# Attention output turned and added tile by tile; the second expert's slots placed later

## The reference

```python
# x, ctx: (8, 256, 512); 32 heads of 8 rows
kv  = einsum("bhil,bhjl->bijhl", ctx, ctx)             # all pairs of a head's rows
y   = irfft(rfft(kv, 1024) * rfft(taps, 1024))[:512] + kv * D
out = einsum("bijhl,bhil->bjhl", y, layernorm(x))      # weighed with the query, summed
x   = x + out
t   = layernorm(x)                                     # 2048 tokens of 512
w, i = top_4(softmax(t @ gate_w.T)); w = w / w.sum()   # 16 experts
buf  = the first 256 tokens that chose each expert     # "slots"
y    = scatter_add(w * (silu(t[buf] @ w_gate) * (t[buf] @ w_up)) @ w_down)
x    = x + y + (silu(t @ sw_gate) * (t @ sw_up)) @ sw_down
```

## Time and profile before

| What | Value |
|---|---|
| median of 3 runs | 621.06 us |
| the profiled execution | 620.51 us |
| its span of instructions | 618.4 us, so 2.1 us lie around it |
| mean granted clock of PE | 0.989 |
| PE busy | 586.6 us (95%), 4387 matmuls |
| DVE busy | 487.8 us (79%) |
| POOL busy | 396.7 us (64%) |
| ACT busy | 291.6 us (47%) |
| group 0's heads summed (`oT` of head 3 done) | 43.6 us |
| PE starts the last group's `mixed_out` | 344.3 us |
| PE starts `gate_up(7, 0)` | 354.3 us |
| PE starts `expert_gu(0, 0, 0)` | 384.5 us |
| one expert, from there on | about 14.05 us |

### The profile page before, as it was taken

The page is one execution under the profiler, slowest core; times in us unless marked ns, Lnnn a source line. Parts: engine busy times, 40 slices in busy tenths (PEclk is TensorE's granted clock), DMA queues, the critical chain, the costliest instruction groups (busy, mean ns, idle before and its releaser), DMA issues.

```text
span 618.4 us, 13645 instructions
## 1 busy us (share of the span) xinstructions
PE 586.6 (95%) x4387; PEld 549.2 (89%) x4387; DVE 487.8 (79%) x1277; ACT 291.6 (47%) x521; POOL 396.7 (64%) x502
## 2 busy tenths in 40 slices
PE   3969999999999999999999999999999999999993
PEld 3759988999999989989999797999999999999992
DVE  6988787679779779598698878988888788887640
ACT  2525334434434435345261333666665566566741
POOL 6997988878888888789771363178834433333342
PEclk9989999999999999999999999999999999999997
DMA  6575215136325336152340146778887888888643
GB/s 189 182 249 170 72 69 166 49 85 179 82 80 156 75 93 170 42 140 55 85 111 2 51 160 209 231 246 233 222 239 211 216 237 237 240 226 241 147 53 48
DMA packets 60489, 92.01 MB, mean 149 GB/s; under 512 B 4260, under 2 KB 36004, under 8 KB 60440
## 3 DMA queue, kind: packets, MB, share of 16 engines
q1 hardware_dynamic: 53168, 74.53, 39.4%
q0 software_dynamic: 7168, 16.78, 13.3%
q10 hardware_dynamic: 104, 0.08, 0.1%
HBM read 74.29 MB, written 17.08 MB: 148 GB/s over the span
## 4 chain that ended last, share of the span: by engine, by line
PE 76%; DVE 9%; POOL 6%; issue 4%; ACT 2%; DVEq 1%; DMA 1%; POOLq 0%; SPq 0%; ACTq 0%
PE gu L678 16%; PE gu L827 15%; PE yb L558 11%; PE mb L844 10%; PE gu L716 7%; PE yb L827 6%; PE mb L530 4%; POOL kv L1230 3%; PE yb L530 2%; PE yb L608 2%; DVE oT L1507 2%; DVE prod L1489 2%; DVE prod L1491 1%; POOL kvl L1247 1%; PE yb L798 1%
## 5 line engine op out<-in xcount | busy, mean ns | idle before, releaser
L678 PE MATMUL gu<-xT,sw 128*128 128x256 f32 (+2 forms) x1104 | 136.4, 281 | 0.3 <-issue 0.3
L678 PEld LDWEIGHTS gu<-xT,sw 128*128 128x128 f32 (+2 forms) x1104 | 131.8, 180 | 1.0 <-issue 0.7
L1230 POOL TENSOR_TENSOR kv<-kT 128x256 f32 (+3 forms) x232 | 106.8, 500 | 0.0
L1247 POOL TENSOR_TENSOR kvl<-kv,kvh 128x1440 fp32r<-128x1440 f32 (+1 forms) x28 | 87.7, 3132 | 25.8 <-ACT kvh L954 25.6
L1489 DVE TENSOR_TENSOR prod<-yb,qT 128x64 f32<-128x64 f32 (+10 forms) x272 | 74.8, 286 | 16.4 <-PE yb L608 11.4
L954 ACT ACTIVATE kvh<-kv 128x1440 fp32r<-128x1440 f32 (+1 forms) x28 | 37.5, 1339 | 78.9 <-POOL kv L1237 36.9
L1507 DVE TENSOR_REDUCE oT<-prod 128x256 f32<-128x2048 f32 x32 | 73.0, 2280 | 0.1
L558 PE MATMUL yb<-kvh,tlast 128*128 128x288 f32 x280 | 66.0, 297 | 0.0
L1491 DVE TENSOR_TENSOR prod<-yb,qT 128x96 f32<-128x96 f32 (+10 forms) x238 | 64.2, 270 | 0.0
L844 PE MATMUL mb<-ed,midh 128*128 128x512 f32 x180 | 57.4, 400 | 0.0
L1776 DVE TENSOR_TENSOR ew<-raw_w,ew 128x704 fp32r<-128x704 f32 x64 | 55.1, 882 | 0.3 <-ACT ew L1102 0.3
(11 more groups left out here) (219 smaller groups left out, 1327.4 us busy)
## 6 DMA issues: line engine op xcount, KB each, us to landing
raw_w<-in_L_ffn_w_gate_dram SPq DMA_DIRECT2D x16, 704.0 KB, 7.9
raw_w<-in_L_ffn_w_up_dram SPq DMA_DIRECT2D x16, 704.0 KB, 8.8
raw_d<-in_L_ffn_w_down_dram SPq DMA_DIRECT2D x16, 512.0 KB, 4.3
tlast<-toeplitz_taps SPq DMA_DIRECT2D x20, 384.0 KB, 3.5
tstep<-tap_steps SPq DMA_DIRECT2D x20, 256.0 KB, 4.1
c_t<-in_ctx_dram SPq DMA_DIRECT2D x16, 256.0 KB, 4.8
x_t<-in_x_dram SPq DMA_DIRECT2D x16, 256.0 KB, 4.9
toep<-toeplitz_taps SPq DMA_DIRECT2D x8, 512.0 KB, 3.9
```

Of the source, the lines that this page charges most:

```text
L678: last = pe.matmul(bank[0:m, u * GT:(u + 1) * GT], sw[:, c, a, col:col + m], xT[:, c, b, :], start=(c == 0 and (a, b) == PASSES[0]), stop= ...
L1230: last = pool.tensor_tensor(to[:, :, POFF[d]:POFF[d] + w], src[:, :, 0:w], src[:, :, d * B:HD * B], ALU.mult)
L1247: pool.tensor_tensor(kvl[:, s, 0:nb, :], kv[:, s, 0:nb, :], kvh[:, s, 0:nb, :].bitcast(fp32), ALU.subtract)\
```

## The change

`mixed_out` waits for half of a group's heads before each tile instead of for all of them before both. In the last group tile 0 is transposed ahead of the convolution of the last head (head 31), and DVE adds x to it and takes its first statistics ahead of that head's `multiply`; tile 1 is transposed behind the first 5 of the 17 matmuls of `down(6, [0])`. In group 0 DVE makes the same two steps one behind the other, tile by tile. The statistics of a group are combined once tile 1's are there.

Further on `slots(1)` moves on PE behind the whole of `down(7, [0])` and the first 8 matmuls of `down(7, [1])`. On DVE `one_hot(1)` moves behind the last low part of the shared expert (`low_mid(7, 5)`), `decode(1, 1)` moves behind `chunk_sum(7, [0])`, and `middle(7, 4)` changes places with `low_mid(7, 3)`. Since `mid` has two buffers, `middle` of the last group now also waits for the low part that read its buffer.

```diff
-            def mixed_out(g, nq):
-                pe.wait_ge(d_sum, GH * (g + 1))
-                for t in range(TT):
+            def mixed_out(g, nq, tiles=range(TT)):
+                for t in tiles:
                     wait(pe, q_ev, TT * nq + t + 1)
+                    pe.wait_ge(d_sum, GH * g + (t + 1) * GH // TT)
                     last = transposes(mb[:, t, :], ...)
                     last.then_inc(o_tr, 1)
...
@@ PE, steps(g)
                     gate_up(g - 1, 3)
+                if not prep:
+                    mixed_out(g, g, [0])
                 convolve(GH * g + 3, 3)
@@ PE, behind the groups
-            mixed_out(NG - 1, NG - 1)
-            down(NG - 2, [0])
+            down(NG - 2, [0], range(-1, 1))
+            mixed_out(NG - 1, NG - 1, [1])
+            down(NG - 2, [0], range(1, SJ - 1))
             down(NG - 2, [1], range(-1, 2))
...
             gate_up(NG - 1, 5)
-            slots(1)
             down(NG - 1, [0])
             down(NG - 1, [1], range(-1, 2))
+            slots(1)
             rows_t(0, 0)
@@ DVE, stats and add_x take tiles
-                for t in range(TT):
+                for t in tiles:
                     dve.bn_stats(st[:, t, :], tile(t))
+                if TT - 1 not in tiles:
+                    return
...
-                dve.wait_ge(x1_ok, TT * g + TT)
+                dve.wait_ge(x1_ok, TT * g + tiles[-1] + 1)
@@ DVE, middle
+                if last_group and i > 3:
+                    dve.wait_ge(last_l, i - 3)
@@ DVE, first_steps
-                add_x(0)
+                add_x(0, [0])
+                add_x(0, [1])
@@ DVE, steps(g)
+                    if hl == 2 and not prep:
+                        add_x(g, [0])
@@ DVE, behind the groups
-            add_x(NG - 1)
+            add_x(NG - 1, [1])
...
             rank_of(2, E)
-            one_hot(1)
             middle(NG - 1, 3)
             low_mid(NG - 1, 2)
+            middle(NG - 1, 4)
             low_mid(NG - 1, 3)
-            decode(1, 1)
-            middle(NG - 1, 4)
             low_mid(NG - 1, 4)
             middle(NG - 1, 5)
             low_mid(NG - 1, 5)
+            one_hot(1)
             low_w(0, 0, 2)
             low_w(0, 0, 3)
             chunk_sum(NG - 1, [0])
+            decode(1, 1)
             places(2, 4)
             values(2, 4)
             places(4, 10)
```

More of the change, by code:

```diff
@@ L1439, in split_shared, with stats @@
                     last.then_inc(sw_l, 1)
-            def stats(tile, st, mv, ve, nm, signal):
-                for t in range(TT):
+            def stats(tile, st, mv, ve, nm, signal, tiles=range(TT)):
+                for t in tiles:
                     dve.bn_stats(st[:, t, :], tile(t))
+                if TT - 1 not in tiles:
+                    return
                 dve.drain()
@@ L1509, in add_up, with add_x @@
                     .then_inc(d_sum, 1)
-            def add_x(g):
+            def add_x(g, tiles=range(TT)):
                 if isinstance(g, int) and g == 0:
@@ L1519, in add_x @@
                     dve.tensor_tensor(x1_tile(g, t), mb[:, t, ::-1], x_tile(g, t), ALU.add).then_inc(x1_ok, 1)
-                dve.wait_ge(x1_ok, TT * g + TT)
+                dve.wait_ge(x1_ok, TT * g + tiles[-1] + 1)
                 wait(dve, t_rs, g)
                 dve.tensor_copy(carrier_d[:, 0:1], carrier_d[:, 1:2])
-                stats(lambda t: x1_tile(g, t), tstat, tmv, tve, tnm, t_stat)
+                stats(lambda t: x1_tile(g, t), tstat, tmv, tve, tnm, t_stat, tiles)
             def low_tokens(g):
```

## The result

| | before | after |
|---|---|---|
| median of 20 runs each | 621.13 us (620.12 to 621.83) | 622.33 us (620.77 to 623.08) |
| the profiled execution | 620.51 us | 620.86 us |
| its span | 618.4 us | 618.9 us |

The ratio is 1.0016, 95% interval [1.001, 1.0022]: 1.2 us slower in the median. That is within the 0.2% called no change ahead, but the interval lies above 1. The forecast was 621.4 us. The profiled execution shows only +0.35 us; it is one of the 6 lowest of its 20, which lie at 620.8 to 621.6 us, while the other 14 lie at 621.9 to 623.1. So this trace shows the instructions' part of the difference, and not all of it. From about L740 on, lines in the changed kernel are numbered 2 to 10 higher.

A forecast was written before the change was run, and what follows sets the result against it. PE was taken as the bound, running three quarters of the chain. Terms -0.5 + 0 - 0.65 + 1.45 = +0.3 us on the profiled 620.51 us gave 620.8, or 621.4 us beside the runs' median; range 619.3 to 623.2 us.

The forecast's parts named there:

- Group 0: 43.6 to 97 us: tile 0 transposed in PE's idle time, POOL starts 1.3 us earlier; -0.5 us, bounds 0 and 1.3.
- The loop: Loop and other groups: one more wait a tile in mixed_out, hidden by queued matmuls; 0, at worst 0.6 us.
- The last group: Its start, 344 to 354 us: DVE finishes tile 1's statistics earlier, so gate_up(7, 0) starts earlier; -0.65 us.
- early terms: The gains forecast ahead of gate_up(7, 0): -0.5 us in the first group, -0.65 us at the last group's start.
- The down projection and expert 0: 371 to 384 us: DVE's moved work delays low_rows(0, 0), and PE idles 2.25 us before expert 0; +1.45 us.
- The second gather: Behind decode(1, 1): starts 6 us later, lands by 391.4 us, before rows_t(1, 1) at 392, so nothing waits.
- The rival of the clock: PE's gap ahead of expert 0: the granted clock falls, costing 0.7 to 2.4 us, 623.0 us; chance 0.25.
- DVE keeps up: Ahead of expert 0: PE's readiness, not low_rows(0, 0), sets the start; -1.95 us, 619.1 us; chance 0.15.

The follow-up runs named there:

- the tiles alone: Kernel before with only the tile by tile transposes and additions, the router's tail left as before: 619.41 us, ratio 0.9979.
- group 0 kept busy: Changed kernel plus 27 unread matmuls on PE in group 0's wait between the two tiles' transposes: 622.29 us.
- the tail alone: Kernel before with only the later slots(1), one_hot(1), decode(1, 1) and earlier middle(7, 4): 623.13 us, ratio 1.0036.
- the one with both gaps filled: Changed kernel plus 27 unread matmuls in group 0's wait and eight in PE's gap ahead of expert 0: 620.75 us.
- the one with the expert's gap filled: Changed kernel plus eight unread matmuls in PE's gap ahead of expert 0: 621.0 us, ratio 1.001.
- the order with filled idle times: Changed kernel with places moved into DVE's two idle times and low rows right behind the decoding: 619.1 us, ratio 0.9975.

## Why the prediction was right, and where it was not

The forecast was 621.4 us in a range of 619.3 to 623.2 us, and 622.33 us was measured. The steps of the instructions came out nearly as added up; two sizes did not, that of the first groups and that of the clock.

- **Group 0**, -0.5 us. The step held: tile 0 at 39.14 (39.3 foretold), POOL's `trs` 1.35 us earlier (1.3), PE's own 0.40 us at the first `gate_up` (0.4). The term was too small in this pair, -1.0 us: "a little more where it waits for POOL and ACT at 87 and 96 us" was 0.6 us, since POOL's low part came 1.02 us earlier and PE's wait of 0.71 us for it at 88 us is gone. It differs between executions. Where the clock in group 0 is back at 50.0 or 49.7 us and not at 48.5, some 0.4 us of it are missing: from tile 0's transposes to `gate_up(7, 0)` it is 314.1 us in these two traces of the changed kernel and 313.75 in the first.
- **The loop**, 0. Right: the shift is 1.02 us both at 86 us (POOL's `low_mid`, 86.02 against 87.04) and at 280 us.
- **The last group**, -0.65 us. It gave -0.4. On the clock of before (the trace's times + 1.02) tile 1 is turned at 345.13 (344.85 foretold) and added at 345.77 (345.6), 0.2 to 0.3 us late. `down(6, [0])` started after an idle time of 0.29 us: the code lets its first piece wait for POOL's low part, which ran at 342.05 for 0.74 us. The sum of the early terms, -1.15 us, stands beside -1.36 us measured with the tiles alone.
- **The down projection and expert 0**, +1.45 us. On the clock of before (the trace's times + 1.40) the middles of tiles 3 to 5 are at 373.16, 375.02 and 376.27 (foretold 373.1, 375.0, 376.2), and `low_rows` at 384.65 (384.65). PE was ready 0.2 us later than foretold, after a wait of 0.55 us for a middle's rounded half, which I had not in the sum; the gap was 2.14 us (2.25), and the term +1.59.
- **The second gather** was covered, as foretold: issued at 382.07 us, 383.47 on the clock of before (383.5), and its rows are transposed at 390.88 without a wait.
- **The rival of the clock**, chance 0.25, price 0.7 to 2.4 us. This is the step that was mis-sized. Its place was right, and 1.6 us taken is near the 1.5 us by which the 48 matmuls grew; that was partly luck, since the forecast's upper bound came from 4.8 us at half the clock behind the wait of group 0, and behind this gap it was 3.4 us. But the clock is lost in more than half of the executions where it could be told (7 of 12 with group 0 kept busy, 5 of 9 with the tail alone), and by the mean clocks in most of the changed kernel's, and so it moves the median. Without it the changed kernel would be where the one with both gaps filled is, at -0.1 us to before, or the one with the expert's gap filled, +0.2; the sum said +0.3. With it, it is +1.0 to +1.3. The forecast counted it as one case of four for the whole kernel, where it is a draw in each execution: the median then goes to the likelier side. The number 621.4 us was 0.9 us short, for this reason as far as the medians show.
- **DVE keeps up** was wrong as the change is written, and is what the order with filled idle times makes true: 29.78 us of stretch, 619.1 us.

So the change consists of a gain of 1.4 us and a loss of 2.4 us (the medians of its two parts alone). Of the loss, 1.6 us are DVE's work moved from idle times into a chain without room, and 0.8 us, by the medians, the clock behind the wait that this made.

## What to carry to other kernels

Before a step is moved, add up what its engine does between the new place and the next thing that it releases; work that sat in the engine's waiting times is free there and costs its whole length where there are none. Fill such waiting times with work that is not urgent (the places here) before moving what is urgent. In this kernel a wait of TensorE of 2 us cost its length and, in a part of the executions, 1.5 us more; look at the spread and at the mean clock of all executions, since the one that was profiled may be the one without it, and since a high time can have another cause.

## What the runs showed of the hardware

- The clock can fall after PE has taken up work again: in the tail alone the gap of 2.17 us ended at 385.94, and the granted clock was 1.00 until 386 us and 0.50 from about 386.4 us on. In the other two traces with a fall (gaps of 2.14 and 2.74 us) it came about 0.4 and 0.2 us behind the end of the gap. Work that is already running did not keep it.
- The same gap costs nothing or 1.5 us. With 2.14 us it was lost in 7 of 12 executions, going by their times and mean clocks, with 2.74 us in 5 of 5, and with 0.37 us in at most one of 11.
- In group 0 of the changed kernel the clock is back at about 48.5 us in one execution, at 49.7 in another and at 50.0 in a third, and in the latter two what follows is some 0.4 us later. With PE kept busy there it stays at 1.00, and what follows comes no earlier (309.0 us from tile 1's transposes to `gate_up(7, 0)`, against 308.8).
